# A first attention layer and a sparse layer: two programs with a barrier between them, or one program of two interleaved step sequences

## The chip, the cores and the metric

The kernel runs on one core of a Trainium2 chip. The metric is the device time of one execution in microseconds (us). PE is TensorE, DVE is VectorE, ACT is ScalarE, POOL is GpSimd, and SP is SyncE, whose queue issues every DMA spoken of here. Each engine takes its own instructions in order, and engines wait for each other by semaphores. TensorE's clock is granted at one of two levels, 1.2 and 2.4 GHz; the profile gives the granted clock of a stretch as a share of full speed.

## The reference, cut to what matters

Eight sublayers add to the state `x` (8 batches of 128 rows of 512). The change touches the first two:

```python
x = x + _L0_xattn_ref(_layernorm(x), ctx_4096, ctx_4096, Wq, Wk, Wv, Wo)   # 32 heads of 16, 8 key heads, softmax
x = x + _L0_ffn_ref(_layernorm(x), c1_w, c2_w, w1, w2t)

def _L0_ffn_ref(x, c1_w, c2_w, w1, w2t):          # INTER = 1792, blocks of 32, rank 16
    inter = xf @ c1_w.T @ c2_w.T                  # rank-16 scores of all 1792 units
    idx = argmax of each block of 32              # one winner of each of 56 blocks
    h = relu(einsum(w1[idx], xf))
    out = einsum(h, w2t[idx])
```

The kernel doesn't gather. It computes all 1792 hidden units, and a mask from the rank-16 scores keeps the first winner of each block. Every product is made of f16 pairs (high and low part), three matmuls each. What follows (a second attention, and so on) is the same before and after.

## The kernel before, in words

**Attention** (`first_attention`). 64 units of work (8 batches of 8), numbered t = 0 to 63; the loops run from t = -16 to 91, since each kind of work has an offset from its unit. Unit t: scores on PE, maxima on DVE (L620), four exponentials on ACT (L489), the high part on DVE (L627) or ACT (L497), the low part on POOL (L716), one DMA transpose from SP's queue (L329), and the mixing matmuls with V seven units later (operand `a_p_t`). Per batch: rows of the next queries are normalised, split and turned; the heads are divided (L633, L637), split (L645 DVE, L721 POOL), turned (L336) and projected (`project_out`, 12 matmuls, operand `a_wo_hi`); DVE adds the result to `x` (L649) and takes statistics (L99).

Near its end this stage already prepares the next: for batches 0 to 3 it normalises the rows (L563, L583), splits them (L706) and turns them (L322), and it loads and splits the two small weights (`Front`).

**Between the stages** stands `end_stage`: semaphores are cleared and all engines meet (L104).

**Sparse layer** (`blocks_ffn`). Its order is written out by tables. 28 tiles: the 14 column tiles of the hidden layer for batches 0 to 3 (tiles 0 to 13) and again for 4 to 7 (tiles 14 to 27). Step t does on PE: `up(t)`, 12 matmuls of 512 columns; `first_of_block(t)`, one matmul that finds the first winners from the turned mask (L2307, called "side" here); the scores of the picks that table `PICK` puts there (L2284, one matmul); `compress(b)` by table `CX` (12 matmuls of 128 columns, operand `f_c_hi`); and `down(t - LAG)`, 12 matmuls, with LAG = 2. ACT makes `first` from side (L2355), DVE multiplies it into `h` (L2414), ACT and DVE split `h` (L2361, L2419). A pick is two DVE instructions (L2402, L2404) and one DMA transpose (L2238). ACT (L2339, L2340) and POOL (L2470) split the weights, in pieces of two tiles. Rows of batches 4 to 7 are normalised at steps 2 to 5 (`NORM`) and compressed at steps 4 to 7 (`CX`). The picks (b, 0) that tile 14 needs stand at steps 8 to 11.

Four PSUM banks are a ring for up, side, pick scores and compressed rows, in the order of use; four hold the sums of `down`. Each step's work waits in order behind that of the step before.

Of the kernel before, what the change touches and what calls it, by code (L numbers as in the profile page):

```python
# [8 lines left out]
P = 128  # L9
B = 8  # L10
# [3 lines left out]
WS = 64.0  # L14

# [158 lines left out]
class Front:  # L174

    AHEAD = B // 2

    def __init__(self, K, stack, c1, c2, w1, w2):
        sb = lambda n, shape, dt: stack.enter_context(K.nc.sbuf_tensor(f"f0_{n}", shape, dt))  # L180
        self.c1, self.c2, self.w1, self.w2 = c1, c2, w1, w2
        self.rank, self.hidden = c1.shape[1], w1.shape[1]
        self.nc1, self.nc2 = sb("nc1", [P, KT, self.rank], F32), sb("nc2", [self.rank, self.hidden], F32)
        self.c1_p, self.c2_s = (sb("c1_hi", [P, KT, self.rank], F16), sb("c1_lo", [P, KT, self.rank], F16)), sb("c2_s", [96, self.hidden], F16)
        self.n1, self.n2 = sb("n1_first", [P, KT, 2 * P], F32), sb("n2_first", [P, 2, DIM], F32)
        self.mv, self.rstd = sb("mv", [P, B, 2], F32), sb("rstd", [P, B], F32)
        self.first_in = K.nc.alloc_semaphore(name="f0_first_in")

    def small(self, kind):
        if kind == "c1":  # L190
            return [t[:, :, :] for t in self.c1_p], self.nc1[:, :, :]
        return [self.c2_s[r:r + self.rank, :] for r in (0, 64, 32)], self.nc2[:, :]

    def load_small(self, sp, small_in):
        sp.dma_start(self.nc1[:, :, :], self.c1.rearrange("(k p) r -> p k r", p=P)).then_inc(small_in, 16)
        sp.dma_start(self.nc2[:, :], self.c2).then_inc(small_in, 16)

    def load_first(self, sp):
        sp.dma_start(self.n1[:, :, :], self.w1.rearrange("(k p) f -> p k f", p=P)[:, :, 0:2 * P]).then_inc(self.first_in, 16)
        sp.dma_start(self.n2[:, :, :], self.w2.rearrange("(f p) d -> p f d", p=P)[:, 0:2, :]).then_inc(self.first_in, 16)  # L200

def first_attention(K, front, x_in, ctx_t, keep_in, wq, wk, wv, wo):
# [20 lines left out]
    LOAD_SMALL, MEAN_FRONT, CLEAR_FRONT, HIGH_FRONT, LOW_FRONT, LOAD_FIRST = TOTAL - 14, TOTAL + 1, TOTAL + 2, TOTAL + 3, TOTAL + 10, TOTAL + 14  # L224
    AHEAD = {B: TOTAL + 2, B + 1: TOTAL + 3, B + 2: TOTAL + 11, B + 3: TOTAL + 12}
    with ExitStack() as c:
        sb = lambda n, shape, dt: c.enter_context(nc.sbuf_tensor(f"{N}_{n}", shape, dt))
        pair = lambda n, shape: (sb(n + "_hi", shape, F16), sb(n + "_lo", shape, F16))
        ring_of = lambda n, k, shape, dt: [sb(f"{n}{i}", shape, dt) for i in range(k)]
        sem = lambda n: K.sem(f"{N}_{n}")  # L230
        nat = {"wq": sb("nq", [P, KT, DIM], F32), "wk": sb("nk", [P, KT, P], F32), "wv": sb("nv", [P, KT, P], F32),
               "wo": sb("no", [P, KT, DIM], F32)}
        w_p = {k: pair(k, list(t.shape)) for k, t in nat.items()}
        mv, rstd = sb("mv", [P, B, 2], F32), sb("rstd", [P, B], F32)
        keep = sb("keep", [P, KV, P], F16)
# [3739 lines left out]
```

## Time and profile before

| | us |
|---|---|
| median of 3 runs | 1521.06 (1518.81 to 1524.52) |
| span of the profiled execution | 1519.0 |
| TensorE busy in the span | 1394.3 (92%) |
| VectorE busy | 1080.1 (71%) |
| GpSimd busy | 718.3 (47%) |
| mean granted TensorE clock | 0.969 |

The span is the time from the first to the last instruction of one profiled execution; the page gives no other time for that execution. Busy time says what an engine did, not what set the end: for this change the stretch from 110 to 352 us of the span matters.

### The profile page before, as it was taken

The page shows a single profiled execution, that of the slowest core. Times are in us where ns is not written, and L with a number is a line of the kernel's source. Part 1 is how long each engine was busy: PE and PEld are TensorE (multiplying, and loading weights), DVE is VectorE, ACT ScalarE, POOL GpSimd, SP SyncE. Part 2 cuts the span into 40 slices and gives each one's busy share as a digit, 9 for nine tenths or more (in the row PEclk, how much of TensorE's full clock was granted, in tenths as well). Part 3 has the DMA queues.
Part 4 walks back from the last instruction along what each step waited for, and adds up shares of the span by engine and source line. Part 5 has one row for each costly group of instructions (what it writes and reads, how often), then busy time and mean ns, then how long its engine had stood idle before and what let it go on. Part 6 is the DMA issues. An engine that isn't in the chain of part 4 may idle for free. (4 is left out here: it accounts for less than half of the span.)

```text
span 1519.0 us, 31488 instructions
## 1 busy us (share of the span) xinstructions
PE 1394.3 (92%) x11352; PEld 830.9 (55%) x11352; DVE 1080.1 (71%) x2125; ACT 762.1 (50%) x2476; POOL 718.3 (47%) x748
## 2 busy tenths in 40 slices
PE   5798599997999999887999999999999788889998
PEld 4676244445777777444655555555555335434444
DVE  7997665645666666667989888898877779966212
ACT  4777363222434432347666666666665457655111
POOL 4888551001433434845666666665665306734000
PEclk9999799999999999999999999999999898989999
DMA  7999572215999988766775655655545401546000
GB/s 189 186 174 181 124 171 42 35 35 122 174 195 184 170 142 136 127 144 147 154 150 112 113 115 111 140 109 115 105 79 79 123 3 32 127 84 112 17 12 28
DMA packets 524570, 174.63 MB, mean 115 GB/s; under 512 B 482576, under 2 KB 507600, under 8 KB 524416
## 3 DMA queue, kind: packets, MB, share of 16 engines
q1 hardware_dynamic: 524416, 172.62, 59.0%
q8 instruction: 92, 1.51, 0.4%
q14 instruction: 62, 0.51, 0.1%
HBM read 53.27 MB, written 2.10 MB: 36 GB/s over the span
## 5 line engine op out<-in xcount | busy, mean ns | idle before, releaser
L1946 POOL TENSOR_TENSOR a_q_ss<-a_q_ss,half 128x4 f32<-128x4 f32 x64 | 90.1, 1408 | 167.6 <-DVE a_q_ss L1855 84.0
L67 PE MATMUL bank<-a_wq_hi,xn_pair 128*128 128x512 f16 (+1 forms) x384 | 140.8, 367 | 10.9 <-DVE a_kn L1860 5.2
L1768 ACT ACTIVATE a_probs<-a_masked,a_negmax 128x128 f32<-128x128 f32 x256 | 99.6, 390 | 101.6 <-DVE a_negmax L1826 101.6
L1285 POOL TENSOR_TENSOR a_p_hl<-a_probs,a_p_hl 128x512 f16<-128x512 f32 x64 | 74.3, 1162 | 142.3 <-DVE a_p_hl L1209 142.3
L68 PE MATMUL bank<-a_wq_lo,xn_pair 128*128 128x512 f16 (+1 forms) x384 | 140.5, 366 | 0.0
L69 PE MATMUL bank<-a_wq_hi,xn_pair 128*128 128x512 f16 (+1 forms) x384 | 140.3, 365 | 0.0
L67 PE MATMUL bank<-a_wo_hi,a_o_hi 128*128 128x512 f16 x256 | 97.8, 382 | 4.4 <-DVE x_state L1842 3.5
L68 PE MATMUL bank<-a_wo_lo,a_o_hi 128*128 128x512 f16 x256 | 97.7, 382 | 0.0
L69 PE MATMUL bank<-a_wo_hi,a_o_lo 128*128 128x512 f16 x256 | 97.5, 381 | 0.0
L1961 POOL TENSOR_TENSOR a_normal<-a_probs,a_recip 128x512 f32<-128x512 f32 x64 | 90.2, 1410 | 5.0
L716 POOL TENSOR_TENSOR a_p_hl<-a_probs,a_p_hl 128x512 f16<-128x512 f32 x64 | 78.0, 1230 | 23.6 <-DVE a_p_hl L627 16.7
L67 PE MATMUL bank<-a_k_t,a_q_t 128*128 128x128 f16 (+1 forms) x384 | 81.1, 237 | 3.8 <-DMA a_q_t<-a_q_nat 3.0
L489 ACT ACTIVATE a_probs<-bank,a_negmax 128x128 f32<-128x128 f32 x256 | 72.6, 382 | 18.3 <-DVE a_negmax L620 17.9
L69 PE MATMUL bank<-a_k_t,a_q_t 128*128 128x128 f16 (+1 forms) x384 | 81.0, 237 | 0.0
L68 PE MATMUL bank<-a_k_t,a_q_t 128*128 128x128 f16 (+1 forms) x384 | 81.0, 237 | 0.0
L1202 DVE TENSOR_REDUCE a_negmax<-bank 128x2 f32<-128x512 f32 x64 | 42.9, 690 | 50.7 <-PE bank L69 50.7
L1823 DVE TENSOR_TENSOR a_masked<-bank,a_mask 128x512 f32<-128x512 f32 x64 | 44.1, 689 | 47.3 <-PE bank L69 47.2
L3796 DVE SCALAR_TENSOR_TENSOR f_h<-bank,f_h 128x512 f32<-128x512 f32 (+1 forms) x22 | 15.2, 689 | 86.3 <-PE bank L69 76.7
L1779 ACT ACTIVATE a_o_hi<-bank 128x512 f16<-128x512 f32 x64 | 38.1, 595 | 66.6 <-PE bank L69 66.6
L1129 ACT ACTIVATE a_probs<-bank,a_negmax 128x256 f32<-128x256 f32 x128 | 53.3, 472 | 33.0 <-DVE a_negmax L1202 33.0
L1954 POOL TENSOR_TENSOR a_recip<-a_total,minus_one 128x4 f32<-128x4 f32 x64 | 64.9, 1013 | 5.6 <-ACT a_probs L1768 5.6
L1736 ACT ACTIVATE a_qn<-bank 128x128 f32<-128x128 f32 x256 | 67.0, 287 | 0.2 <-DVE a_q_nat L1873 0.2
(467 smaller groups left out, 5022.4 us busy)
## 6 DMA issues: line engine op xcount, KB each, us to landing
a_no<-in_L_xattn_Wo SPq DMA_DIRECT2D x9, 1024.0 KB, 5.7
a_nq<-in_L_xattn_Wq SPq DMA_DIRECT2D x8, 1024.0 KB, 5.8
a_n_wq<-in_L_xattn_Wq SPq DMA_DIRECT2D x4, 768.0 KB, 5.7
a_n_wo<-in_L_xattn_Wo SPq DMA_DIRECT2D x4, 768.0 KB, 6.1
a_nk<-in_L_xattn_Wk SPq DMA_DIRECT2D x9, 256.0 KB, 3.0
a_nv<-in_L_xattn_Wv SPq DMA_DIRECT2D x9, 256.0 KB, 3.1
f_v_hat<-in_L_ffn_w SPq DMA_DIRECT2D x2, 1152.0 KB, 6.2
x_state<-in_x SPq DMA_DIRECT2D x8, 256.0 KB, 5.2
```

Source lines behind the costliest of these rows:

```text
L67: pe.matmul(out, lh, rh, start=start, stop=False)
L68: pe.matmul(out, lh, rl, start=False, stop=False)
L69: return pe.matmul(out, ll, rh, start=False, stop=stop)
L489: m = act.activation(probs[t % PS][:, h * P:(h + 1) * P], s_bank[t][:, h * P:(h + 1) * P], ACT.Exp, bias=negmax[t % 4][:, h:h + 1])
L716: pool.tensor_tensor(p_hl[t % PS][:, 1, :], probs[t % PS][:, :], p_hl[t % PS][:, 0, :], ALU.subtract).then_inc(plo_done.sem, 1)
L1129: m = act.activation(probs[u % PROBS][:, n, :], s_bank[(s, t)][:, n * KTL * P:(n + 1) * KTL * P], ACT.Exp, bias=negmax[u % 4][:, n:n + 1])
L1285: pool.tensor_tensor(p_hl[s % PN][:, 1, t, :], probs[unit(s, t) % PROBS][:, :, :].rearrange("p h n -> p (h n)"), p_hl[s % PN][:, 0, t, :], ...
L1736: m = act.activation(dst[:, h, :], src[:, h, :], ACT.Square, scale=1.0 / WS, accum_out=sums[:, h:h + 1])
L1768: m = act.activation(probs[s % 2][:, h, :], src, ACT.Exp, bias=negmax[s % 2][:, h:h + 1], accum_out=total[s % 2][:, h:h + 1])
L1946: pool.tensor_tensor(r[:, :], r[:, :], K.half[:, 0:n], ALU.pow).then_inc(root_done.sem, 1)
L1954: pool.tensor_tensor(recip[s % 2][:, :], total[s % 2][:, :], K.minus_one[:, :], ALU.pow).then_inc(recip_done.sem, 1)
L1961: m = pool.tensor_tensor(normal[s % 2][:, t, :, :], probs[s % 2][:, :, t * P:(t + 1) * P], by, ALU.mult)
```

## The change

One program in place of two. `Front` and the preparation inside the attention go away. Both functions now return a `Stage` of five generators, one for each engine, which yield after each step, and `side_by_side` runs them in turn: attention step t, then sparse step t - 78. The attention ends at t = 91, and the sparse layer begins at its own step -30, which is t = 48. The barrier between them is gone.

```diff
+BESIDE = 78
+def in_turn(a, b, shift, program_a, program_b):
+    for t in range(min(a.first, b.first + shift), max(a.end, b.end + shift)):
+        if a.first <= t < a.end:
+            next(program_a)
+        if b.first <= t - shift < b.end:
+            next(program_b)
...
 def stage_0_to_1(K, a, early):
     with ExitStack() as c:
-        front = Front(K, c, *(a[f"L0_ffn_{w}"] for w in ("c1_w", "c2_w", "w1", "w2t")))
-        first_attention(K, front, a["x"], a["ctx_t"], a["keep"], *(a[f"L0_xattn_{w}"] for w in ("Wq", "Wk", "Wv", "Wo")))
-        K.end_stage()
-        blocks_ffn(K, front, early)
-        K.in_use.append(front.first_in)
+        attention = first_attention(K, c, a["x"], a["ctx_t"], a["keep"], *(a[f"L0_xattn_{w}"] for w in ("Wq", "Wk", "Wv", "Wo")))
+        blocks = blocks_ffn(K, c, attention, *(a[f"L0_ffn_{w}"] for w in ("c1_w", "c2_w", "w1", "w2t")), early)
+        side_by_side(K.nc, attention, blocks, BESIDE)
```

The tables of the sparse layer:

```diff
-    FIRST, LAG, RING, MASKS = -16, 2, 2, 4
-    NORM = {4: 2, 5: 3, 6: 4, 7: 5}
-    CX = {0: -9, 1: -8, 2: -7, 3: -6, 4: 4, 5: 5, 6: 6, 7: 7}
-    PICK = {(b, i): (4 * i - 5 if i else -7) + b if b < HALF else 4 * (i + 1) + b for b in range(B) for i in range(PARTS)}
+    FIRST, LAG, RING, MASKS = -30, 4, 2, 4
+    LOAD_SMALL, LOAD_FIRST, LOAD_SECOND, MEANS, SMALL_HIGH, SMALL_LOW, LATER = -29, -28, -9, -22, -12, -9, 4
+    ROWS = {0: -13, 1: -12, 2: -11, 3: -10, 4: 5, 5: 6, 6: 7, 7: 8}
+    CX = {b: ROWS[b] + (4 if b < HALF else 1) for b in range(B)}
+    PICK = {(b, i): (4 * i - 5 if i else -8) + b if b < HALF else (4 * (i + 1) if i else 6) + b for b in range(B) for i in range(PARTS)}
```

In the attention, the projection and the addition of the last batch come at t = 80 and 81 (before: 79 to 82, and 84):

```diff
+    LAST_OUT, LAST_ADD = TOTAL + 16, TOTAL + 17
+    out_at = lambda t, k: [b for b in at(t, OUT + k) if b < B - 1] + ([B - 1] if t == LAST_OUT else [])
```

The buffers of the sparse layer are laid over ones that the attention has done with (`placed`, at the offsets in `over.place`), with a wait for the last use of each, as `all_scored`, `all_mixed`, `all_projected` or `probs_turned`. Its PSUM ring takes banks 5, 7, 0, 1, and its sums banks 2, 3, 4, 6, each after the attention's last use (`bank_over`). The high and low parts of a weight piece are now tensors of their own.

The order of instructions moves at three places on which the prediction rests. In the names, `a0_` belongs to the attention and `f0_` to the sparse layer.

POOL, at t = 48 to 52 of the attention. Before:

```order
L716 TENSOR_TENSOR a0_p_hl5<-a0_probs5,a0_p_hl5 128x512
L721 TENSOR_TENSOR a0_o_hl0<-a0_o_nat0,a0_o_hl0 128x512
L716 TENSOR_TENSOR a0_p_hl6<-a0_probs6,a0_p_hl6 128x512
L716 TENSOR_TENSOR a0_p_hl0<-a0_probs0,a0_p_hl0 128x512
L716 TENSOR_TENSOR a0_p_hl1<-a0_probs1,a0_p_hl1 128x512
```

The same place in the changed kernel:

```order
L688 TENSOR_TENSOR a0_p_hl5<-a0_probs5,a0_p_hl5 128x512
L693 TENSOR_TENSOR a0_o_hl0<-a0_o_nat0,a0_o_hl0 128x512
L2560 MEMSET f0_cx_s_66 96x1024
L2562 MEMSET f0_c2_s_52 96x1792
L2563 MEMSET f0_before 128x128
L2565 AFFINE_SELECT f0_before<-f0_before 128x128
L2569 AFFINE_SELECT f0_before<-f0_before 128x128
L2572 AFFINE_SELECT f0_before<-f0_before 128x128
L688 TENSOR_TENSOR a0_p_hl6<-a0_probs6,a0_p_hl6 128x512
L688 TENSOR_TENSOR a0_p_hl0<-a0_probs0,a0_p_hl0 128x512
```

Six instructions that make constants now stand inside the attention's main phase, between the low parts of units 47 and 48.

SP's queue, from the heads of batch 6 to the masks of the first four picks. Before, up to the barrier:

```order
L336 DMA_TRANSPOSE a0_o_t0<-a0_o_hl0 128x8x128
L322 DMA_TRANSPOSE xn_pair<-a0_xn_hl0 128x8x128
L322 DMA_TRANSPOSE xn_pair<-a0_xn_hl1 128x8x128
L336 DMA_TRANSPOSE a0_o_t1<-a0_o_hl1 128x8x128
L322 DMA_TRANSPOSE xn_pair<-a0_xn_hl0 128x8x128
L322 DMA_TRANSPOSE xn_pair<-a0_xn_hl1 128x8x128
L199 DMA f0_n1_first<-in_L0_ffn_w1 128x4x256
L200 DMA f0_n2_first<-in_L0_ffn_w2t 128x2x512
```

In the changed kernel:

```order
L346 DMA_TRANSPOSE a0_o_t0<-a0_o_hl0 128x8x128
L2274 DMA_TRANSPOSE xn_pair<-f0_xn_hl0_62 128x8x128
L2274 DMA_TRANSPOSE xn_pair<-f0_xn_hl1_63 128x8x128
L2274 DMA_TRANSPOSE xn_pair<-f0_xn_hl2_64 128x8x128
L2274 DMA_TRANSPOSE xn_pair<-f0_xn_hl3_65 128x8x128
L2267 DMA f0_n1_1_56<-in_L0_ffn_w1 128x4x256
L2267 DMA f0_n2_1_57<-in_L0_ffn_w2t 128x2x512
L2283 DMA_TRANSPOSE f0_mask_t_71<-f0_mask0_67 128x4x128
L2283 DMA_TRANSPOSE f0_mask_t_71<-f0_mask1_68 128x4x128
L2283 DMA_TRANSPOSE f0_mask_t_71<-f0_mask2_69 128x4x128
L346 DMA_TRANSPOSE a0_o_t1<-a0_o_hl1 128x8x128
L2283 DMA_TRANSPOSE f0_mask_t_71<-f0_mask3_70 128x4x128
```

The heads of batch 7 (`a0_o_t1`) now stand among the first masks, and the first weight pieces are loaded at t = 50.

DVE, where batch 4 is normalised among the tiles. Before, from its rows (after tile 2) to `h` of tile 4; its compressed rows (`f0_cx_s`) come four rows further on:

```order
L2375 TENSOR_SCALAR f0_xn0<-x_state,f0_mv,f0_rstd 128x512
L2378 CAST f0_xn_hl0<-f0_xn0 128x512
L2402 TENSOR_REDUCE f0_top3<-bank5 128x16
L2404 TENSOR_TENSOR f0_mask3<-bank5,f0_top3 128x512
L2414 SCALAR_TENSOR_TENSOR f0_h1<-bank6,f0_first1 128x512
L2419 SCALAR_TENSOR_TENSOR f0_h_lo0<-f0_h1,f0_h_hi0 128x512
L2375 TENSOR_SCALAR f0_xn1<-x_state,f0_mv,f0_rstd 128x512
L2378 CAST f0_xn_hl1<-f0_xn1 128x512
L2402 TENSOR_REDUCE f0_top0<-bank4 128x16
L2404 TENSOR_TENSOR f0_mask0<-bank4,f0_top0 128x512
L2414 SCALAR_TENSOR_TENSOR f0_h0<-bank5,f0_first0 128x512
```

In the changed kernel, from its rows (after tile 5) to its compressed rows (in step 6):

```order
L2450 TENSOR_SCALAR f0_xn0_58<-x_state,f0_mv,f0_rstd 128x512
L2453 CAST f0_xn_hl0_62<-f0_xn0_58 128x512
L2479 TENSOR_REDUCE f0_top2<-bank0 128x16
L2481 TENSOR_TENSOR f0_mask2_69<-bank0,f0_top2 128x512
L2491 SCALAR_TENSOR_TENSOR f0_h0<-bank1,f0_first0 128x512
L2496 SCALAR_TENSOR_TENSOR f0_h_lo1<-f0_h0,f0_h_hi1 128x512
L2450 TENSOR_SCALAR f0_xn1_59<-x_state,f0_mv,f0_rstd 128x512
L2453 CAST f0_xn_hl1_63<-f0_xn1_59 128x512
L2479 TENSOR_REDUCE f0_top3<-bank7 128x16
L2481 TENSOR_TENSOR f0_mask3_70<-bank7,f0_top3 128x512
L2469 SCALAR_TENSOR_TENSOR f0_cx_s_66<-bank0,f0_cx_s_66 16x128
```

Between a batch's rows and their use by `compress` there were two tiles, and now there is one.

## Rows read from the trace of the kernel before

**Rows 1.** Busy time by stretch: stretch, length, busy PE, PEld, DVE, ACT, POOL, clock, DMA.
```profile
110.00:142.50 32.50, 31.08 (x479) 24.83 (x476) 28.50 (x54) 26.11 (x87) 27.95 (x24) 1.00 1.17 175
142.50:188.60 46.10, 26.84 (x197) 12.76 (x198) 27.20 (x52) 17.91 (x33) 25.59 (x25) 0.74 0.65 135
188.60:345.80 157.20, 155.80 (x756) 71.39 (x757) 84.15 (x143) 55.27 (x84) 32.80 (x21) 1.00 0.33 70
```
**Rows 2.** Timeline of PE: start, us, what, count [idle before, releaser].
```profile
172.78 0.26 PE L67 MATMUL bank<-xn_pair,f_c_hi 128*16 128x128 f16 x1 [4.26 <-PEq L2266]
...
177.16 0.22 PE L67 MATMUL bank<-xn_pair,f_c_hi 128*16 128x128 f16 x1
...
177.33 0.22 PE L67 MATMUL bank<-xn_pair,f_c_hi 128*16 128x128 f16 x1
...
188.62 0.38 PE L2307 MATMUL bank<-f_mask_t,f_before 128*128 128x512 bf16 x1 [1.35 <-DMA f_mask_t<-f_mask]
```
**Rows 3.** Timeline of SP's queue after the last unit of the attention.
```profile
151.96 1.28 SPq L336 DMA_TRANSPOSE a_o_t<-a_o_hl  x1
154.51 4.28 SPq L322 DMA_TRANSPOSE xn_pair<-a_xn_hl  x2
```
**Rows 4.** DMA issues, 125 to 345 us: queue, count, size, median us to landing.
```profile
f_n<-in_L_ffn_w SPq DMA_DIRECT2D x3, 512.0 KB, 5.0
...
f_mask_t<-f_mask SPq DMA_TRANSPOSE x32, 2.5
a_p_t<-a_p_hl SPq DMA_TRANSPOSE x16, 3.5
...
xn_pair<-f_xn_hl SPq DMA_TRANSPOSE x8, 3.2
```
**Rows 5.** Timeline of POOL from the attention's last units to the first picks.
```profile
145.98 3.56 POOL L716 TENSOR_TENSOR a_p_hl<-a_probs,a_p_hl 128x512 f16<-128x512 f32 x3 [0.63 <-ACT a_p_hl L497]
149.50 1.15 POOL L721 TENSOR_TENSOR a_o_hl<-a_o_nat,a_o_hl 128x512 f16<-128x512 f32 x1
...
150.94 1.04 POOL L753 TENSOR_TENSOR f_rstd<-f_rstd,half 128x4 f32<-128x4 f32 x1
...
154.43 1.58 POOL L757 MEMSET f_c_s<- 96x1792 f16 x1
...
171.54 0.95 POOL L2472 MEMSET f_cx_s<- 96x1024 f16 x1 [4.60 <-POOLq L104]
...
179.65 0.29 POOL L2494 TENSOR_SCALAR_AFFINE_SELECT f_before<-f_before 128x128 bf16<-128x128 bf16 x1
```
**Rows 6.** Waits of SP's queue, 100 to 152 us: total, times, longest.
```profile
SPq L329 <- POOL a_p_hl L716: 19.6, 19, 2.1
```
**Rows 7.** Timeline of DVE: a split cast beside a POOL memset, and two picks.
```profile
153.51 2.79 DVE L583 CAST a_xn_hl<-a_xn 128x512 f16<-128x512 f32 x1
...
182.94 0.69 DVE L2402 TENSOR_REDUCE f_top<-bank 128x16 f32<-128x512 f32 x1
...
184.50 0.69 DVE L2402 TENSOR_REDUCE f_top<-bank 128x16 f32<-128x512 f32 x1
```
**Rows 8.** Timelines of ACT, DVE, POOL and SP's queue at tile 2.
```profile
197.62 0.57 ACT L2355 ACTIVATE f_first<-bank 128x512 f32<-128x512 f32 x1
...
199.66 0.80 DVE L2419 SCALAR_TENSOR_TENSOR f_h_lo<-f_h,f_h_hi 128x512 f16<-128x512 f32 x1 [0.69 <-ACT f_h_hi L2361]
...
200.95 0.43 DVE L2378 CAST f_xn_hl<-f_xn 128x512 f16<-128x512 f32 x1
...
201.46 1.16 POOL L2464 TENSOR_TENSOR f_xn_hl<-f_xn,f_xn_hl 128x512 f16<-128x512 f32 x1 [1.55 <-DVE f_xn_hl L2378]
...
202.64 1.24 SPq L2231 DMA_TRANSPOSE xn_pair<-f_xn_hl  x1
```
**Rows 9.** Timeline of DVE: `h` of two tiles without picks.
```profile
329.81 0.69 DVE L2414 SCALAR_TENSOR_TENSOR f_h<-bank,f_first 128x512 f32<-128x512 f32 x1 [3.32 <-ACT f_first L2355]
...
335.20 0.69 DVE L2414 SCALAR_TENSOR_TENSOR f_h<-bank,f_first 128x512 f32<-128x512 f32 x1 [3.31 <-ACT f_first L2355]
```

More of the change, by code:

```diff
@@ new lines, in first_attention @@
+    pieces = [("wk", 0)] + [("wq", i) for i in range(4)] + [("wv", 0)] + [("wo", i) for i in range(4)]
+    whi_done, wlo_done = Steps(sem("whi"), pieces), Steps(sem("wlo"), pieces)
+    per_batch = lambda n: Steps(sem(n), batches)
+    per_unit = lambda n: Steps(sem(n), units)
+    stats_done, mean_done, root_done = sem("stats"), sem("mean"), sem("root")
+    chi_done, clo_done = (per_batch(n) for n in ("chi", "clo"))
+    xn_done, xhi_done, xlo_done = (per_batch(n) for n in ("xn", "xhi", "xlo"))
@@ new lines, in first_attention, with weights_split, rows_used @@
+    stage = Stage(FIRST, END, sync, tensor, scalar, vector, gpsimd)
+    stage.place, stage.taken = place, taken
+    last, final = B - 1, TOTAL - 1
+    def weights_split(engine):
+        engine.wait_ge(wlo_done.sem, len(pieces))
+    def rows_used(engine):
+        engine.wait_ge(clo_done.sem, clo_done.count(last))
+        engine.wait_ge(xlo_done.sem, xlo_done.count(last))
+        for b in (last - 1, last):
+            landed(engine, xt_in, b)
+        engine.wait_ge(q_bank.filled(last), q_bank.n_filled(last))
@@ new lines, in blocks_ffn @@
+    xn, xn_hl = ([on_rows[f"{n}{i}"] for i in range(HALF)] for n in ("xn", "xn_hl"))
+    top = ring_of("top", MASKS, [P, SPAN * P // BLK], F32)
+    first_f, h = ring_of("first", 2, [P, HT], F32), ring_of("h", 2, [P, HT], F32)
+    h_hi, h_lo = ring_of("h_hi", LAG + 1, [P, HT], F16), ring_of("h_lo", LAG + 1, [P, HT], F16)
+    tiles, batches, ahead = list(range(TILES)), list(range(B)), list(NEXT)
+    live = lambda t: [t] if 0 <= t < TILES else []
+    at = lambda table, t: [use for use, when in table.items() if when == t]
@@ new lines, in blocks_ffn, with weight @@
+    cxhi_done = Steps(sem("cxhi"), batches)
+    parts = sorted(PICK, key=PICK.get)
+    top_done, pick_done = Steps(sem("top"), parts), Steps(sem("pick"), parts)
+    xt_in, mask_in = [sem(f"xt_in{b}") for b in batches], [sem(f"mask_in{m}") for m in range(MASKS)]
+    hhi_done, hlo_done = Steps(sem("hhi"), tiles), Steps(sem("hlo"), tiles)
+    down_done = Steps(sem("down"), [u for u in tiles if u % NT < NT - 1])
+    of_half = lambda u: range(HALF * (u // NT), HALF * (u // NT) + HALF)
+    def weight(use):
+        kind, q = use
+        return [p[:, :, :] for p in w_p[use]], nat[kind][q % RING][:, :, :]
```

1680 lines of the change are left out of this document (850 added, 830 removed).

## The prediction, made before the changed kernel was run

> **What bounds the kernel now.** I read the page first, then busy time by stretch, then each engine's timeline around the seam of the two stages, then the DMA table. The reader is to see three stretches [rows 1]. From 110 to 142.5 us, the last third of the attention, PE, DVE and POOL are all between 86 and 96% busy at full clock. From 142.5 to 188.6, the seam, PE is busy for only 26.84 of 46.10 us, and at a mean clock of 0.74. From 188.6, where the first side matmul starts [rows 2], to 345.8, where the last `down` ends, PE is busy for 155.80 of 157.20 us at clock 1.00: PE alone bounds it. What comes after 345.8 starts at a barrier in both kernels, so it keeps its length, and the whole effect is the shift of the last `down`.
>
> PE's price is read from two tiles without picks, 335.20 - 329.81 = 5.39 us for 25 matmuls, or 0.216 us each [rows 9]. An `up` or a `down` is 12 x 0.216 = 2.6 us. A compress at full clock is 4 x 0.17 = 0.7 us, from two starts three matmuls apart [rows 2].
>
> **Term 1: the first side matmul comes earlier.** Before, compress(0) started at 172.78 and side(0) at 188.62, 15.8 us later [rows 2]. Between them lie the chain compress, ACT, DVE, score, pick, mask transpose of four batches. All its inputs were there, so 15.8 us is the chain itself at this place, and the changed kernel runs the same one. What changes is when it can begin. In SP's queue the rows of batch 0 now stand directly behind the heads of batch 6. That transpose ends its issue at 151.96 + 1.28 = 153.2 [rows 3]. The rows don't hold it up: their means and roots are made at t = 56 now (before, POOL made the root at 150.94 to 152.0 [rows 5], and DVE waited for it), and POOL reaches them right behind the heads of batch 6, at 150.65, so that their low part is ready at 151.8. A transpose of rows lands in 3.2 us [rows 4]: compress(0) starts at 156.4. Four rows follow each other in the queue at 1.3 us, faster than four compresses with their picks take. The chain gets longer at one place: the heads of batch 7 stand in SP's queue before the fourth mask, one issue of 1.3 us, which DVE and POOL have ready only just in time. So side(0) starts at 156.4 + 15.8 + 1.2 = 173.4, against 188.62: 15.2 us gained. The barrier and the wait for the first weights are part of it (the pieces are loaded 20 us earlier). up(0) stands before side(0) in both kernels and is inside the 15.8 us, part of it at the lower clock (mean 0.74 in the seam [rows 1]).
>
> **Term 2: the last projection moves among the tiles.** Before, it ran ahead of the barrier; now it stands at t = 80, behind tile 1, where PE has no gap: 2.6 us lost. Since `down` waits four steps, tiles 0 to 3 need only 14 matmuls each, 3.0 us of PE. DVE needs 3.8 us for such a step (`h` and its low part about 2.2 with the gap for ACT, a pick 1.56 [rows 7]). But the ring lets PE go a tile ahead, and the projection and down(0) fill what is left; followed step by step, down(0) ends 17.2 us behind side(0), about the sum of its matmuls. I cost this at nothing; if that cover fails it is at most 4 x 0.8 = 3.2 us.
>
> **Term 3: the attention ends later.** Six POOL instructions now stand between units 47 and 48: two memsets and four small ones. The memsets took 1.58 and 0.95 us and a small one 0.29 [rows 5]: 1.58 + 0.95 + 4 x 0.29 = 3.7 us, and the root adds 1.0 at t = 56. SP's queue is nearly always waiting for POOL's low parts there, 19 waits of 19.6 us in all [rows 6], so POOL paces the transposes, and PE and then DVE follow. SP gets two loads of 512 KB between units 48 and 49, which land in 5.0 us against 3.5 of a transpose [rows 4]. Both ends: nothing, if the idle time of POOL absorbs it (32.50 - 27.95 = 4.6 us [rows 1], with the last three low parts waiting for ACT anyway [rows 5]); or 3.7 + 1.0 + 5.0 = 9.7 us, if nothing is absorbed. The nearest row is POOL's idle time, nearly as long as its new work, so I take a value near the low end: 2 us lost.
> The split cast at 153.51 took 2.79 us, with the memset beside it from 154.43 to 156.01, where the one after it took 0.43 in other places [rows 5, 7, 8]. By that rule the memsets, moved from the seam into the full attention, hold DVE's casts for up to their own length, and the sum would lose some 2 us more. The trace agrees with the rule for this cast; I leave my value, since it lies in the bounds.
>
> **Term 4: the rows of batches 4 to 7 are late.** The tables give `compress(b)` one tile after the rows (before: two). The chain was measured at tile 2 [rows 8]: from 197.62, when ACT starts `first` just behind side, to 202.64, when the transpose is issued, 5.0 us, and 3.2 to landing: 8.3 us, with side's end. PE, from the end of side(5), has a score, down(1), up(6), side(6) and a score before compress(4): 27 matmuls, 5.8 us. It then stands still for 2.5 us. For the next batch the interval holds that stall and a compress: 5.8 + 0.7 + 2.5 = 9.0, no wait. For batch 6 it is 6.5 against 8.4, 1.9 us; for batch 7 none. Together 4.4 us lost. Before, with two tiles between, there was none.
>
> **Term 5: the mask of tile 14 is late.** The pick (7, 0) now stands in step 13, behind `h` of tile 13 and another pick (before: step 11). From side(13): 2.9 us to the low part of `h` (197.62 to 200.46, plus the start [rows 8]), two picks 3.1, the transpose 2.5 [rows 4]: 8.5 us. PE has two scores, down(9) and up(14), 26 matmuls, 5.6 us. side(14) waits 2.9 us.
>
> **Sum.** -15.2 + 2.6 + 2.0 + 4.4 + 2.9 = -3.3 us. The profiled span of 1519.0 becomes 1515.7. The page gives no other time of that execution; the median of the runs is 2.1 above its span, so the time is 1521.1 - 3.3 = 1517.8, taken as 1517.5.
>
> **Rivals.**
> A. The tiles don't stall. If DVE and SP get ahead of PE (a transpose sooner, PE slower at half clock somewhere), terms 4 and 5 vanish: -15.2 + 2.6 + 2.0 = -10.6, 1510.5; with the attention unmoved, 1508.5. For it: PE was 99% busy over 28 tiles before, with picks and rows between [rows 1]. Against it: the stalls follow from the order and measured durations alone.
> B. Slower: the attention is late by the upper bound. The loads and constants stand before a chain where POOL paces SP and SP paces PE, and the lag of seven units gives no more than it needs. At 9.7 us instead of 2, the sum is +4.4: 1525.5. It decides from 5.3 us of delay on. Against it: the stretch after t = 56 has idle time on every engine [rows 1].
> C. The tiles don't start so early, since compress(0) stands before the last mixing matmuls in PE's order, and the last heads wait behind that and behind the first picks on DVE, and the fourth mask behind the heads on SP. 5 us more in this loop give 1522.5.
>
> **How the numbers follow.** The forecast has a chance of 0.55, A 0.28, B 0.08, C 0.09. Faster or slower means by over 0.5%, 7.6 us, about what a measurement of this kernel can tell from no change: below 1513.5 or above 1528.7. Faster is A and an eighth of the forecast, 0.35. Slower is the far side of B and C, 0.05. The rest is 0.60. The forecast's own range, from the bounds of term 3 and a few us on term 1, is 1513 to 1521. To hold 8 in 10 it reaches to most of A and into B and C: 1508.5 to 1523.
>
> **What would show it.** The stretch from side(0) to the last `down` should be 157.2 + 2.6 + 7.3 = 167 us long, with PE idle before compress(4) and compress(6) for the landing of rows, and before side(14) for that of a mask. side(0) should start near 175.5 (173.4 and 2 of delay). The last unit's low part on POOL should end 1 to 3 us behind 149.5. If that comes more than 5 us late, term 3 is wrong; if PE has no idle time among the tiles, terms 4 and 5 are; if side(0) is later than 179, term 1 is.

## The result and the profile after

| | before | after |
|---|---|---|
| median (lowest to highest), us | 1520.35 (1518.81 to 1524.52, 4 runs) | 1528.67 (1527.19 to 1530.29, 4 runs) |
| ratio after / before, 95% interval | | 1.0055 (1.0036 to 1.0074) |
| profiled execution: span, mean clock | 1519.0, 0.969 | 1526.0, 0.967 |
| first side matmul (weight load) | 188.58 | 184.22 |
| first add behind the last `down` | 345.74 | 352.60 |

The changed kernel is slower by 0.55%. The forecast was 1517.5, with a range up to 1523. Every ratio in this document leaves out two executions that fell far above the others of their kernel, one of e7 (1684.65 us) and one of e9 (2864.02 us). In the profiled executions the last `down` comes 6.9 us later and the span is 7.0 us longer, so in this pair what stands behind the last `down` took as long, and the stretches ahead of it hold the effect. Busy time by stretch, columns as in [rows 1]: the last third of the attention, the seam to the first side matmul, and the tiles.

```profile
110.00:142.50 32.50, 26.57 (x375) 19.93 (x373) 25.37 (x49) 21.43 (x71) 27.13 (x27) 0.88 1.09 179
142.50:184.20 41.70, 26.46 (x287) 15.77 (x285) 32.56 (x52) 23.07 (x51) 28.13 (x19) 0.81 0.82 150
184.20:352.60 168.40, 159.12 (x754) 72.85 (x768) 85.06 (x149) 55.18 (x84) 33.44 (x23) 0.99 0.29 65
```

In the same 32.5 us of the attention PE does 375 matmuls where it did 479, at clock 0.88 and not 1.00 [rows 1]; the tiles take 168.4 us where they took 157.2. The first row is the stretch of term 3, which the prediction put at 2.0 us.

The attention is late. POOL's timeline from the heads of batch 4 to the attention's last units, against [rows 5]:

```profile
124.49 1.35 POOL L693 TENSOR_TENSOR a_o_hl<-a_o_nat,a_o_hl 128x512 f16<-128x512 f32 x1
125.78 0.94 POOL L2560 MEMSET f_cx_s<- 96x1024 f16 x1
126.67 1.58 POOL L2562 MEMSET f_c_s<- 96x1792 f16 x1
...
129.62 6.90 POOL L688 TENSOR_TENSOR a_p_hl<-a_probs,a_p_hl 128x512 f16<-128x512 f32 x6
137.84 1.15 POOL L688 TENSOR_TENSOR a_p_hl<-a_probs,a_p_hl 128x512 f16<-128x512 f32 x1 [1.32 <-DVE a_p_hl L609]
...
154.18 3.75 POOL L688 TENSOR_TENSOR a_p_hl<-a_probs,a_p_hl 128x512 f16<-128x512 f32 x3 [0.64 <-ACT a_p_hl L499]
```

The last low part ends at 157.9, 8.4 us behind 149.5. POOL works off six low parts in a row behind its constants, and then it waits for DVE: the engines wait for each other in a loop, and the delay has gone around it. DVE's timeline in that place, maxima of the scores:

```profile
136.74 0.69 DVE L602 TENSOR_REDUCE a_negmax<-bank 128x4 f32<-128x512 f32 x1 [2.85 <-PE bank L70]
142.05 0.69 DVE L602 TENSOR_REDUCE a_negmax<-bank 128x4 f32<-128x512 f32 x1 [3.38 <-PE bank L70]
```

DVE stood still for 2.85 and 3.38 us for PE. PE and its weight loads, in turn, waited for transposed probabilities. Waits from 110 to 142 us, first of before, then of after (total, times, longest):

```profile
PEld bank L67 <- DMA a_p_t<-a_p_hl: 3.2, 7, 0.9
```

```profile
PEld bank L68 <- DMA a_p_t<-a_p_hl: 7.1, 5, 3.0
```

The seam. Timeline of PE, then of its weight loads, against [rows 2]:

```profile
165.66 0.27 PE L68 MATMUL bank<-xn_pair,f_c_hi 128*16 128x128 f16 x1 [5.11 <-issue]
```

```profile
184.22 0.10 PEld L2361 LDWEIGHTS bank<-f_mask_t,f_before 128*128 128x128 bf16 x1 [3.49 <-issue]
```

From compress(0) to side(0) are 18.6 us, where 15.8 were measured before and 17.0 predicted. The tiles. PE's waits from 205 to 285 us, at the three places that the prediction names:

```profile
214.72 0.22 PE L68 MATMUL bank<-xn_pair,f_c_hi 128*16 128x128 f16 x1 [2.70 <-DMA xn_pair<-f_xn_hl]
229.20 0.22 PE L68 MATMUL bank<-xn_pair,f_c_hi 128*16 128x128 f16 x1 [1.65 <-DMA xn_pair<-f_xn_hl]
```

```profile
PE bank L2338 <- DMA f_mask_t<-f_mask: 3.0, 1, 3.0
```

The last of the three has a second price. PE alone in the 4 us behind that wait (busy PE, clock, DMA share, GB/s):

```profile
267.79:271.79 4.00, 4.00 (x11) 0.57 0.00 0
```

At a clock of 0.57 these 4 us do what 2.3 us do at full clock, so the wait of 3.0 us costs some 4.7.

### The profile page after: what moved, and what is told of

It reads as the page before. It is cut to its first block and busy times, and to the rows that moved or that the text cites. A ratio compares the mean times of both kernels' runs of the same rounds, so it can differ in the third digit from the quotient of the medians.

```text
span 1526.0 us, 31477 instructions
## 1 busy us (share of the span) xinstructions
PE 1392.1 (91%) x11337; PEld 832.0 (55%) x11352; DVE 1082.9 (71%) x2125; ACT 762.7 (50%) x2476; POOL 721.6 (47%) x748
```

## Experiments

Each kernel's profile is one execution, and executions differ. In the fourteen traces of this study, which run the same attention up to t = 48 (but for four small instructions at the start of two), POOL's low part for the heads of batch 4 at t = 49 starts anywhere from 122.7 to 126.2 us (123.20 before, 124.49 after). So I measure the attention's delay from there to the end of its last low part: 26.3 us before, 33.4 after. Of the 8.4 us, 7.1 belong to the change, and 1.3 were there before the first added instruction. This distance has scatter of its own: four kernels with the same order up to the last low part (after, e7, e9, e13) have 33.4, 32.6, 32.5 and 32.5 us, so the 7.1 is 6.1 to 7.1, and a difference below 1 us between two single executions shows nothing. The seam of the same four has 18.6, 18.6, 19.4 and 19.4 us. The expectations below still speak of the plain 157.9, and two of them call the heads batch 5's by mistake. The table has all runs; "heads to last" is that distance, "seam" goes from compress(0) to the weight load of side(0), "tiles" from there to the first add, and "clock" is the mean granted clock of PE in the tiles.

| run | heads to last | compress(0) | seam | side(0) | tiles | clock | time: ratio to before (95%) |
|---|---|---|---|---|---|---|---|
| before | 26.3 | 172.8 | 15.8 | 188.6 | 157.2 | 1.00 | 1 |
| after | 33.4 | 165.7 | 18.6 | 184.2 | 168.4 | 0.99 | 1.0055 (1.0036 to 1.0074) |
| e1: constants late | 32.1 | 165.8 | 19.2 | 185.1 | 168.1 | 0.99 | 1.0027 (1.0012 to 1.0043) |
| e2: loads late | 29.4 | 162.5 | 23.0 | 185.5 | 169.8 | 0.98 | 1.0062 (1.0045 to 1.0079) |
| e3: all late | 28.2 | 160.3 | 22.6 | 182.9 | 174.9 | 0.95 | 1.0049 (1.0034 to 1.0064) |
| e4: before, loads early | 30.5 | 179.7 | 14.6 | 194.3 | 157.2 | 1.00 | 1.0016 (1.0002 to 1.0029) |
| e5: before, POOL work | 29.2 | 175.5 | 16.5 | 192.0 | 157.2 | 1.00 | 1.0013 (1.0001 to 1.0025) |
| e6: loads in pieces | 31.2 | 166.9 | 18.5 | 185.4 | 172.1 | 0.97 | 1.0050 (1.0030 to 1.0070) |
| e7: tables | 32.6 | 164.9 | 18.6 | 183.5 | 161.1 | 1.00 | 0.9987 (0.9969 to 1.0006) |
| e9: down two late | 32.5 | 163.5 | 19.4 | 182.9 | 174.6 | 0.96 | 1.0072 (1.0044 to 1.0100) |
| e10: tables, loads behind the rows | 29.2 | 163.1 | 20.2 | 183.4 | 164.0 | 0.98 | 0.9981 (0.9967 to 0.9996) |
| e11: and constants out | 27.4 | 162.2 | 20.1 | 182.2 | 162.7 | 0.99 | 0.9983 (0.9971 to 0.9994) |
| e12: and mask before heads | 27.0 | 162.6 | 18.8 | 181.4 | 162.5 | 1.00 | 0.9982 (0.9969 to 0.9995) |
| e13: compress two behind | 32.5 | 163.6 | 19.4 | 183.0 | 168.2 | 0.97 | 1.0028 (1.0015 to 1.0042) |

What stands behind the last `down` took 1173.3 us before, and between 1168.5 and 1174.1 in the others' single executions, whose code there is the same; so one span is no measure of 2 us, and the times are read from the ratios. The length of the tiles needs the clock column beside it: at a mean clock of 0.95 some 5% of 174.9 us, 8 to 9 us, go to the clock in e3, where after has under 2. That is nearly all of the 6.5 us between the two.

### What makes the attention late (e1 to e6)

Theories: POOL's constants (P), the two loads of 512 KB (L), or neither (N).

e1, in `gpsimd`:

```diff
-            if t == FIRST + 1:
-                constants()
+            if t == -13:
+                constants()      # the two memsets
+            if t == -8:
+                triangle()       # the four small ones
```

> The changed kernel with POOL's six constant instructions moved out of the attention: the two memsets (0.94 and 1.58 us) to step -13 (t = 65, behind the last low part of the probabilities and the first rows), the four small ones to step -8. Theory P (POOL's constants are the cause, since POOL paces the transposes and its idle time absorbs nothing): the last low part ends 4 to 6 us earlier than 157.9 us, near 153, and the kernel becomes 3 to 5 us faster than the changed one, about 1524. Theory L (the two loads of 512 KB between two transposes are the cause): the last low part stays at 157 to 158, the time within 1 us of the changed kernel. Theory N (neither: the attention was late already before t = 48, by layout or by chance): no change either.

Measured: 1.3 us less (heads to last 32.1, last low part at 156.9), but only 0.4 less than three other executions of the changed kernel's order. So e1 alone doesn't show a cost of the constants. With the loads out of the way it shows better: 29.4 and 29.2 us with the constants there (e2, e10), 28.2, 27.4 and 27.0 without them (e3, e11, e12). The ratio fell by more (1.0027) than the stretch up to the last `down` shows, which was 0.6 us longer in the profiled execution; the intervals of the two ratios overlap, and I read no gain of the seam from it.

e2:

```diff
-    LOAD_SMALL, LOAD_FIRST, ... = -29, -28, ...
+    LOAD_SMALL, LOAD_FIRST, ... = -29, -12, ...
```

> The changed kernel with the two loads of 512 KB (first pieces of w1 and w2) moved from step -28 (t = 50) to step -12 (t = 66), behind the last transposes of probabilities and the rows of batches 0 and 1. Theory L: the last low part on POOL ends 4 to 5 us earlier than 157.9 us, since a load lands in 5.0 us where a transpose takes 3.5 and PE then waits for a transposed unit; time 3 to 5 us below the changed kernel. Theory P: the last low part stays within 1 us of 157.9. Theory N: the same as P.

Measured: the attention gains 4.0 us, as theory L said, and the time gains nothing. The gain was spent in the seam, in a wait that the expectation had not looked for. Timeline of ACT in e2:

```profile
166.35 1.06 ACT L2397 ACTIVATE f_w_hi<-f_n 128x1024 f16<-128x1024 f32 x1 [10.28 <-DMA f_n<-in_L_ffn_w]
```

The split of the first piece of w1 stands at step -10 in ACT's order, ahead of the high part of compress(0) at step -9. It now waited 10.3 us for the late load, and held the chain: the seam took 23.0 us.

e3 has the edits of e1 and e2, and also

```diff
-    LOAD_SMALL, LOAD_FIRST, LOAD_SECOND, MEANS, ... = -29, -28, -9, -22, ...
+    LOAD_SMALL, LOAD_FIRST, LOAD_SECOND, MEANS, ... = -16, -12, -9, -14, ...
```

> The changed kernel with constants and first loads both moved as in the two runs before, and also the small loads (to step -16) and the means and roots of the first four batches (to step -14): nothing of the sparse layer is left between t = 48 and 61. If the work put among the attention's last units is the whole cause, the last low part ends at 149.5 to 150.5 us as in the kernel before, side(0) comes 7 to 8 us earlier (near 176.5) and the time is 7 to 8 us below the changed kernel, near 1521. If the attention is late for another reason (theory N), it ends at 154 or later although nothing stands there. If P and L add up, the gain is the sum of the two runs before; if they share a cover, it is more than that sum.

Measured: 5.3 us of 7.1 given back in the attention, the sum of e1 and e2 (1.3 + 4.0), as closely as the scatter lets one say; the time unchanged. ACT again splits w1 late in the seam (22.6 us), behind a wait of 3.2 us for the load, and the tiles are 6.5 us longer, by the clock (0.95 for 0.99) and a wait for rows of 3.7 us in the place of 2.7. Theory N is out: with the work gone, so is most of the delay. The 1.8 us left are not explained (up to 1 of them may be scatter); the root at t = 64 now stands in front of the last low parts on POOL.

e4, in the kernel before:

```diff
-    ..., LOAD_FIRST = ..., TOTAL + 14
+    ..., LOAD_FIRST = ..., TOTAL - 14
```

> The kernel before, with one thing altered: its two loads of 512 KB are issued at t = 50 and not at t = 78. The loads landed before they were needed in either place as far as the trace shows (the ACT split waits for the barrier), so the seam may get up to 1 us shorter. Theory L: the attention's last low part comes 4 to 5 us behind 149.5 us and the kernel is 3 to 4 us slower than before. Theory P: last low part at 149.5 to 150.5, the time the same or up to 1 us less.

Measured: 4.2 us in the attention (30.5 against 26.3), and 0.16% slower, by its interval 0.3 to 4.4 us. The loads by themselves are a cost, as L said. PE's waits in e4, 110 to 142 us, against 3.2 us and at most 0.9 in before:

```profile
PEld bank L67 <- DMA a_p_t<-a_p_hl: 6.5, 6, 4.4
```

What PE waits for shows in the landings too. Transposes of probabilities in 133 to 137 us, first of before, then of after, where they stand right behind the two loads (count, median us to landing):

```profile
a_p_t<-a_p_hl SPq DMA_TRANSPOSE x4, 4.1
```

```profile
a_p_t<-a_p_hl SPq DMA_TRANSPOSE x2, 5.7
```

In e4 the two in that place took 5.4 us.

e5, in the kernel before: the memset of c2_s at t = 49 and not 66, and there also

```diff
+    pool.memset(front.scrap[:, :], 0.0)       # [96, 1024] f16, read by nothing
+    pool.memset(square[:, :], 1.0)            # [128, 128], and the three affine_selects on it
```

> The kernel before, with the six POOL instructions of the changed one at t = 49: the memset of c2_s moved there from t = 66, a memset of the size of cx_s and the four small ones on a buffer that nothing reads (they are extra work, the real ones stay behind the barrier). From the run that moved them away in the changed kernel (last low part 1.0 us earlier), the last low part ends at 150.5, time within 1 us of before. If the costs don't add (each alone costs more than it gives back when the other stands), it is 2 to 4 us late.

Measured: 2.9 us (29.2 against 26.3), three quarters of the time that the six instructions take, 125.78 to 129.65; the ratio is 1.0013, 0.2 to 3.8 us. The 1.0 us that I had read from e1 was too little. So 4.2 for the loads and 2.9 for POOL, each alone in the kernel before, add up to the 7.1 us of the changed kernel. Each is one execution with scatter of up to 1 us, so that the sum meets 7.1 exactly is luck; that neither was absorbed is shown.

e6, eight loads of 128 KB, one behind each transpose of t = 50 to 57:

```diff
-            if t == LOAD_FIRST:
-                load(("w1", 0))
-                load(("w2", 0))
+            if LOAD_FIRST <= t < LOAD_FIRST + 8:
+                load_first(t - LOAD_FIRST)
```

> The changed kernel with the first pieces of w1 and w2 (1 MB in all) loaded as eight DMAs of 128 KB, one behind each transpose of t = 50 to 57, and not as two of 512 KB in a row. Theory B (the burst is what hurts: a transpose that lands behind 1 MB is late for PE, while 128 KB are absorbed by the lag): the last low part of POOL ends 3 to 6 us earlier than 157.9, as in the run that moved the loads (154.6) or better, and since the split of w1 on ACT no longer waits for a late load (10.3 us idle in that run), the seam keeps its 18.6 us: side(0) near 180, time 3 to 5 us below the changed kernel. Theory V (the bytes themselves cost, since the DMA engines have nothing to spare beside the transposes): the last low part stays within 1 us of 157.9 and the time is unchanged; more issues on SP's queue may even add 1 us.

Measured: 31.2 us, 1.3 to 2.3 back of the 4.0 to 4.2 that the loads cost; the time is unclear against the changed kernel (1.0050 and 1.0055), and the tiles were 3.7 us longer here, at clock 0.97. So part of the cost is the burst: the transposes of 125 to 145 us land in 3.4 us (median) here, in 4.3 in after and in 3.5 in before. That the rest is the bytes is not shown. The DMA engines had time to spare in those 20 us of e6 (share 0.90, 150 GB/s), while SP's queue gave 0.6 to 0.7 us to the issue of each of the eight loads; that SP then was the pace is as good a theory, and wasn't tried. In the kernel before, over 110 to 142.5 us, the 16 engines are at 1.17 of their time, overlapped, with transposes [rows 1]. The same 20 us, 125 to 145, of before and of after (stretch, length, busy PE, PEld, DVE, ACT, POOL, clock, DMA share, GB/s):

```profile
125.00:145.00 20.00, 17.46 (x267) 13.36 (x264) 16.59 (x31) 15.67 (x55) 15.65 (x14) 0.99 1.14 178
```

```profile
125.00:145.00 20.00, 14.88 (x184) 10.41 (x182) 11.11 (x24) 10.89 (x36) 15.92 (x18) 0.74 1.02 182
```

The mean rate is nearly the same, but with 1 MB of loads in it: SP issued 9 transposes of probabilities in these 20 us of after, and 12 in before. PE's 184 matmuls for 267 go with that, and its clock fell to 0.74. The equal rate is no limit: beside the loads, from 136 to 137 us of after, it was 395 GB/s.

### The tiles (e7, e13, e9)

e7:

```diff
-    ..., LATER = ..., 4
-    ROWS = {..., 4: 5, 5: 6, 6: 7, 7: 8}
-    CX = {b: ROWS[b] + (4 if b < HALF else 1) for b in range(B)}
-    PICK = ... (4 * (i + 1) if i else 6) + b ...
+    ..., LATER = ..., 3
+    ROWS = {..., 4: 4, 5: 5, 6: 6, 7: 7}
+    CX = {b: ROWS[b] + (4 if b < HALF else 2) for b in range(B)}
+    PICK = ... (4 * (i + 1) if i else 5) + b ...
```

> The changed kernel with other steps for the tiles: rows of batches 4 to 7 one tile earlier (steps 4 to 7), their compresses two tiles behind them, their first picks one tile earlier (9 to 12). Terms 4 and 5 of the prediction, as the changed kernel's trace shows them (PE waits 4.4 us for rows in two places, 3.0 us for the mask of tile 14), should both go: side(0) to the last down 161 us (168.4 before), time 7 us below the changed kernel, near 1521.5. Rival: the waits are moved and not removed, since DVE is then the one that paces the tiles with picks (two picks in steps 9, 10 and 12): 165 to 167 us, 1 to 3 us gained.

Measured: tiles of 161.1 us, 7.3 less, as the first theory said, and by the two ratios a time 0.7% below the changed kernel, level with the kernel before. The waits that went are 4.4 + 3.0 us, and with the mask's wait went the 1.7 us of half clock behind it; a wait of 1.2 us for `h` came in, and 0.4 us more of waits behind DVE. Busy time by stretch of e7:

```profile
183.50:344.60 161.10, 157.46 (x754) 72.50 (x768) 85.62 (x148) 54.98 (x84) 32.98 (x23) 1.00 0.33 68
```

e13 takes apart what e7 joins:

```diff
-    CX = {b: ROWS[b] + (4 if b < HALF else 1) for b in range(B)}
+    CX = {b: ROWS[b] + (4 if b < HALF else 2) for b in range(B)}
```

> The changed kernel with one number altered: compress(b) of batches 4 to 7 two tiles behind its rows and not one. Term 4 of the prediction alone: PE's 4.4 us of waits for rows (2.7 and 1.7 in the changed kernel) go, the 3.0 us for the mask of tile 14 stay; side(0) to the last down 168.4 - 4.4 = 164 us, time 4 us below the changed kernel, about 1524.5. Rival: the two waits aren't separate, and the time won ahead of tile 14 is given back there, since the mask hangs on DVE's chain and not on PE: the wait for the mask grows to 5 to 7 us, 166 to 168 us in all, 0 to 2 us gained.

Measured: the waits for rows are gone, the one for the mask of tile 14 is still 2.8 us, so the rival, by which that wait grows to 5 to 7 us, is out. The ratio fell from 1.0055 to 1.0028, some 4 us as the theory said, though the two intervals overlap. But the tiles took 168.2 us, not 164. PE's waits in e13 over the tiles:

```profile
PE bank L2361 <- DMA f_mask_t<-f_mask: 2.8, 1, 2.8
PE bank L68 <- DVE f_h L2491: 1.2, 1, 1.2
PE bank L68 <- DVEq L2484: 1.1, 1, 1.1
```

1.2 us came back as a wait for `h`. Most of the rest is the clock of the first 6 us. PE alone, by stretch (busy PE, clock, DMA share, GB/s), of e13 and then of the changed kernel:

```profile
183.00:189.00 6.00, 5.96 (x15) 0.50 1.01 280
```

```profile
184.20:190.20 6.00, 5.73 (x27) 1.00 1.03 287
```

15 matmuls at half clock against 27: 12 x 0.216 = 2.6 us, and 164 + 1.2 + 2.6 = 167.8.

e9:

```diff
-    FIRST, LAG, RING, MASKS = -30, 4, 2, 4
+    FIRST, LAG, RING, MASKS = -30, 2, 2, 4
```

> The changed kernel with down two tiles behind and not four. In PE's order down(0) then stands directly behind the last projection of the attention (both at t = 80), in whose bank it writes its fourth sum; that bank is only free when DVE has added it to x, one step later (t = 81), behind h of tile 2 on DVE. Theory: PE stands still for 4 to 6 us there once, and the time is 3 to 6 us above the changed kernel; so the lag of four pays for itself by this alone. Rival: DVE is early enough there, less than 1 us of difference.

Measured: the wait is there, and it is a little shorter than I said. Timeline of PE in e9:

```profile
198.41 0.39 PE L68 MATMUL bank<-f_w_hi,f_h_hi 128*128 128x512 f16 x1 [2.86 <-DVE x_state L631]
```

down(0) stood 2.9 us for DVE's addition of the last projection. PE alone in the 4 us behind it:

```profile
198.41:202.41 4.00, 4.00 (x12) 0.64 0.56 164
```

The tiles are 6.2 us longer than in after, with a mean clock of 0.96 for 0.99, so the wait was not the whole price. The ratio, 1.0072 from three executions, is above that of the changed kernel by 2.6 us, with overlapping intervals: likely a cost of the order of the wait, not shown by the time alone.

### A version that is faster than both (e10 to e12)

e10 has the tables of e7, and

```diff
-    LOAD_FIRST = -28
-    SPLIT = {("w1", 0): -10, ...}
+    LOAD_FIRST = -10
+    SPLIT = {("w1", 0): -7, ...}
```

> The changed kernel with the tables of the run that gained 8 us in the tiles, and the first two loads of 512 KB behind the rows of all four batches (step -10), with ACT's split of the first piece of w1 moved from step -10 to -7, behind two compresses, so that ACT doesn't wait for the load in front of them. Theory C (the attention and the seam both gain): from the low part of the heads of batch 5 to the last low part of the probabilities 29.4 us as in the run with late loads (33.4 in the changed kernel), the seam 18.6 us or up to 1 us more, side(0) near 180, the last down near 341, time 1515 to 1517. Rival (the load's landing holds what follows in the seam anyway, as the split of w1 and the mask transposes come behind 2 MB of loads): seam 21 to 23 us, side(0) near 184, time the same as with the tables alone, 1519 to 1521.

Measured: 1517.3 us, 0.19% below the kernel before (0.04 to 0.33%), 0.7% below the changed one. The attention gains as in e2. In the seam only ACT's split waits for the load, 1.1 us, behind two compresses. The seam was 20.2 us all the same. PE's mean clock in it was 0.75 (0.82 in the changed kernel), but e11's seam took 20.1 us at 0.83, so the clock is not enough of a reason; that the masks are now transposed behind 2 MB of loads may have a part in it, which was not taken apart. The tiles again began at half clock (0.52, 14 matmuls in 6 us). So it lies between the two cases that were expected; its gain over e7, 0.9 us by the two ratios, is far inside the intervals.

e11 has also the two memsets at step -13 and the four small ones at the start of the kernel (`FIRST = -94`).

> The run with the loads behind the rows, and POOL's constants also out of the attention: the four small ones at the very start of the kernel, the two memsets at step -13. Theory: from the heads of batch 5 to the last low part 28 us (1.3 to 2.9 less than with the loads alone), side(0) 1 to 2 us earlier, time 1 to 2 us below that run. Rival: the memsets in the seam hold DVE's and POOL's rows there and give it back, no difference.

Measured: heads to last 27.4, 1.8 us less than e10, side(0) 1.2 us earlier; no difference in time (1518.0). e12 adds, in SP's queue:

```diff
-            for b in at(t, OSPLIT):
+            for b in at(t, OSPLIT) if t < TOTAL + 8 else at(t - 1, OSPLIT):
                 turn_heads(b)
```

> The same, with one exchange in SP's queue: the fourth mask of the seam before the heads of batch 7. In the changed kernel the heads took SP from 180.21 to 181.44 and the fourth mask was issued at 181.48, though DVE had it at 180.3. Theory (the prediction's 1.2 us for this place): side(0) comes 1.1 to 1.2 us earlier in respect to compress(0), time 1 us less. Rival: the transposes of the heads only trade places with the mask on the way and the last projection is late instead, no difference.

Measured: the seam is 1.3 us shorter than in e11 (18.8 against 20.1), and PE's gap in front of side(0) is 2.2 us and not 3.6, so the exchange did what it was to do. The time is the same (1518.1). The tiles took 162.5 us, as in e11, but at full clock, where e11 lost some 1.6 us to the clock (0.99); against e7, also at full clock, they are 1.4 us longer, with 2.9 us of waits behind DVE for 1.5. So the rival, that the gain is given back further on, is not out. All three are faster than the kernel before by 2 to 3 us with intervals that exclude no change; which is the best, 12 runs each don't tell.

## Why the prediction was wrong

The sum was to be -3.3 us and was +6.9. Term by term, from the table:

- **Term 3 was mis-sized: 2.0 predicted, 7.1 measured** (6.1 to 7.1 by four executions; 8.4 between the two profiled ones, 1.3 of it scatter from before the change, and more than the 5 us that the prediction named as the sign that term 3 is wrong). The step that failed reads "nothing, if the idle time of POOL absorbs it (32.50 - 27.95 = 4.6 us)", and then "the nearest row is POOL's idle time". POOL's idle time was not slack. It is the time in which POOL waits for DVE and ACT, which wait for PE, which waits for transposes that POOL releases: in a loop in which each waits a little for the next, an instruction put on one engine is late for all, and e5 gave 2.9 us for 3.9 us of instructions. The loop is read from the waits; what e5 and e4 show is its price. For the loads (4.2 us by e4) the prediction had set one landing against another, 5.0 and 3.5 us [rows 4], and gave no price to the transposes that stand behind the loads; these landed in 5.4 to 5.7 us where 4.1 were measured before. And the idle time of 4.6 us was POOL's, while the loads don't run on POOL. The mechanism is rival B, which had 0.08, short of its upper bound of 9.7.
- **The weighed rule.** Two subtractions and two casts of DVE in the seam after, the first pair beside POOL's low parts, the second beside none:

```profile
155.54 1.38 DVE L2450 TENSOR_SCALAR f_xn<-x_state,f_mv,f_rstd 128x512 f32<-128x512 f32 x1
156.96 1.26 DVE L2453 CAST f_xn_hl<-f_xn 128x512 f16<-128x512 f32 x1
...
164.42 0.54 DVE L2450 TENSOR_SCALAR f_xn<-x_state,f_mv,f_rstd 128x512 f32<-128x512 f32 x1
164.99 0.43 DVE L2453 CAST f_xn_hl<-f_xn 128x512 f16<-128x512 f32 x1
```

  Each takes 0.8 us longer beside POOL. The Trainium skill, "SBUF — State Buffer", "Who interferes with whom", says that the engine which issues first gets the shared ports for its whole instruction and that the other is blocked; these rows agree. The prediction read its cast of 2.79 us as held by the memset alone. But POOL had a low part under way when the cast began at 153.51 in the kernel before:

```profile
153.09 1.39 POOL L706 TENSOR_TENSOR a_xn_hl<-a_xn,a_xn_hl 128x512 f16<-128x512 f32 x1 [1.12 <-DVE a_xn_hl L583]
```

  The cast waited through that and through the memset that followed it without a gap (154.43 to 156.01), so not all of the 2.36 us is the memset's. Beside the memsets in the attention no cost of its own shows: e5 lost 2.9 us, and the POOL work alone is 3.9.
- **Term 1: the working held, its start and the chain were off.** side(0) at 175.5 was predicted, and measured at 184.2, past the 179 that the prediction had named as its sign. 6.4 us of the 8.7 are the attention's (8.4 - 2.0). compress(0), at 165.7, is 0.9 later than 156.4 + 8.4. The chain is 1.6 longer than 17.0: 1.2 was allowed for the heads ahead of the fourth mask, and e12 gave 1.3. Another 0.9 was not seen: DVE's low part of c2_s stands ahead of the one of compress(0). Timelines of DVE and ACT, after:

```profile
165.59 2.94 DVE L2464 SCALAR_TENSOR_TENSOR f_c_s<-f_nc,f_c_s 16x1792 f16<-16x1792 f32 x1
168.56 0.28 DVE L2469 SCALAR_TENSOR_TENSOR f_cx_s<-bank,f_cx_s 16x128 f16<-16x128 f32 x1
```

```profile
167.41 0.27 ACT L2413 ACTIVATE f_cx_s<-bank 16x128 f16<-16x128 f32 x1
```

  ACT was done at 167.7, DVE came at 168.56. The seam itself is only known to a few us: 14.6, 15.8 and 16.5 with the order of the kernel before (e4, before, e5), 18.6 to 19.4 with that of the changed one. So the heads ahead of the mask are shown by e12, and the 0.9 rests on one execution.
- **Terms 4 and 5 had the waits right, and left out what one of them does to the clock.** 2.5 and 1.9 us before compress(4) and compress(6) were predicted, 2.7 and 1.7 measured; 2.9 for the mask of tile 14, 3.0 measured, and 1.7 more behind it by the clock. e7 made the tiles 7.3 us shorter, the sum of the two terms (4.4 + 2.9), but partly by luck: 1.7 us of half clock behind the mask's wait went too, and some 1.6 us of new waits came. Rival A, no stalls, which I gave 0.28 for the sake of the 99% busy PE of before, was wrong: that order had two tiles of room, this one had one.
- **Term 2 was near.** The tiles of e7, without the stalls, are 3.9 us longer than before, for 2.6 us of projection. The remaining 1.3 may be the wait of 1.2 us for `h`; that was not tried. The changed kernel doesn't have that wait: its 1.3 us over the prediction in the tiles go with the 1.7 us of half clock.

Together: -3.3 predicted, +5.1 of term 3, +1.3 of scatter ahead of the change, +2.5 at compress(0) and in the chain, +1.3 in the tiles by the clock, is +6.9. The median moved by 8.3, which the ratio's interval (5.5 to 11.3 us) holds. The forecast's own number would have been wrong by the first of these alone: with 7.1 in the place of 2.0 the sum is +1.8, outside the 1513 to 1521 that I gave it by a little; the range up to 1523 was passed through the sum of them all. Term 3's bounds were right (0 to 9.7), and the value was taken at their low end though the row beside it showed three engines at 0.86 to 0.96 and the DMA engines above one.

## What to carry to other kernels

Where several engines are each nearly busy and wait for each other by turns, nobody's idle time is free: price added work there near its full length (here 2.9 us for 3.9 us of POOL work), and added loads not by their own landing but by what they do to the transfers behind them (here 4.2 us for 1 MB in a row). Price a wait of PE with the clock behind it. When work is moved earlier in a queue, look at everything it is now in front of; when it is moved later, look at who stands behind the instruction that consumes it, as ACT's split did in e2. The length of a wait worked out from the order and a measured chain was right to 0.2 us here, and one excused by a share of idle time was not.

## What the runs showed of the hardware

The first 6 us of tiles run at the full granted clock (1.00, the level of 2.4 GHz) or down to 0.50 (1.2 GHz), by execution, behind a seam that reads nearly the same. In the 8 us ahead of side(0) PE is busy for 4.0 us in 17 matmuls, and waits some 3.5 us for the mask at its end. PE alone in those 8 us and in the 6 us behind them (busy PE, clock, DMA share, GB/s), of e10 and then of e7:

```profile
175.36:183.36 8.00, 4.01 (x17) 0.93 0.57 86
183.36:189.36 6.00, 5.59 (x14) 0.52 0.96 281
```

```profile
175.53:183.53 8.00, 4.01 (x17) 1.00 0.44 87
183.53:189.53 6.00, 5.75 (x27) 1.00 1.02 276
```

14 matmuls against 27, 13 x 0.216 = 2.8 us. Of the ten kernels with that gap three kept the clock (after, e1, e7), and seven had 0.50 to 0.76. The kernels whose last gap is shorter, 1.8 us (before, e4, e5) and 2.2 us (e12), all had 1.00. Inside the tiles, where PE is busy but for its waits, the clock of the 4 us behind each wait reads as follows:

| PE waited for | us | kernels | clock of the next 4 us |
|---|---|---|---|
| mask of tile 14 | 2.8 to 3.0 | after, e1, e2, e3, e6, e9, e13 | 0.57 to 0.68 in all seven |
| rows of batch 4 | 3.7; 3.2 | e3; e6 | 0.50; 0.66 |
| rows of batch 4 | 2.4 to 2.7 | after, e1, e2; e9 | 1.00 in three; 0.57 in e9 |
| rows of batch 6 | 1.6 to 1.7 | after, e1, e2, e3, e6, e9 | 1.00 in all six |

So a wait of some 3 us in a stretch bound by PE costs what it is, and in most executions half as much again or more in the clock (1.3 us or more of the next 4); waits under 2 us cost only themselves. The gap alone doesn't decide, as the seam's 3.5 us kept the clock in three kernels of ten. Both are told here as what went together; no run changed a gap and nothing else. That may be part of why the gains of e3 and e10 in the attention don't show in the time. One execution each is too little to say how often.
